# Attention: the turned sums and the row of maxima go to ScalarE and GpSimd, two sets of partial maxima, another order of TensorE's steps

## The chip, the cores and the metric

One core of one Trainium2 chip runs the whole program. The metric is the time of the device in microseconds (us) for one execution, a median over runs.

## The reference

A decoder layer on x of shape (1, 2048, 256): causal self-attention with 16 heads of 16, a cross-attention without softmax over 1601 context rows, and a mixture of 8 experts (two chosen per token) beside a shared one; a layer norm stands behind each. The change is in the self-attention alone:

```python
q = (x @ wq + bq).reshape(B, S, H, Dh).transpose(0, 2, 1, 3)
k = (x @ wk + bk).reshape(B, S, H, Dh).transpose(0, 2, 1, 3)
v = (x @ wv + bv).reshape(B, S, H, Dh).transpose(0, 2, 1, 3)
scores = jnp.einsum('bhqd,bhkd->bhqk', q, k) / jnp.sqrt(jnp.float32(Dh))
scores = jnp.where(causal[None, None], scores, jnp.float32(-jnp.inf))
attn = jax.nn.softmax(scores, axis=-1)
out = jnp.einsum('bhqk,bhkd->bhqd', attn, v)
```

S is 2048, H is 16, Dh is 16.

## The kernel before, in words

`project` forms q, k and v and the first maxima, `attend` does the attention of the 16 heads, `finish` the rest. Each is a block of its own; the next begins when every engine has ended the one before.

**The heads.** In `attend` a head's causal scores are cut into ten quads: a block of 512 queries (`qb`) by four tiles of 128 keys (`k0`). Quads 0, 2, 5 and 9 lie on the diagonal. A quad's scores are formed with keys on the partitions, in two halves, A and B. ScalarE turns each half into `probs` (an exponential, L735); on diagonal quads GpSimd zeroes the later keys (L689, `hide_later`). Three quads later (`LAG`) TensorE weighs the values with them (a W step, `weigh`, L792) and sums in `acc`; ScalarE copies `acc` when a block of queries is done (L740). The row of maxima, which keeps the exponential small, is a 49th row of the stacked q (`qstack`), so the scores of head h + 1 need it there first.

**The maxima.** For them the scores are formed once more, with queries on the partitions, in 35 pieces of up to 512 columns. Each piece takes a bank of a ring of three (`ring`, `NRING`); VectorE reduces it into `partial` (L178), and when the last piece of a head is in, reduces `partial` into `neg_max` (L871). Since there is one `partial`, it waits for its own `neg_max` before it takes a piece of the next head. TensorE transposes `neg_max` (M, L827), VectorE scales it into `max_row` (L876), and SP sends it by two DMAs into `qstack` (L667). Pieces of quads 6 to 9 belong to the head after next, the others to the next.

**The sums.** A head's four `acc_sb` blocks are folded by TensorE into a bank of the ring (F, L800, which ScalarE copies into `folded`, L747), transposed into another (T, L807), and normalised by VectorE: a reciprocal of the sums (L857) and a product into `attn` (L859).

**The order.** `STEPS` has one string a quad and is TensorE's order: A and B are the two halves of the scores, W a weighing of the quad three back, M, F, T as above, and small letters are pieces: w a whole one of 512 columns, n one of 384, d a whole one at the diagonal, p two of 256, q four of 128. M, F, T and the pieces go through the ring in that order: each waits until the bank three entries back has been read (`wait_taken`). VectorE takes its entries in the same order. TensorE works in two row groups (partitions 0 to 63 and 64 to 127) for scores and pieces, so that two of them can run beside each other; `given` picks the group for a piece.

**GpSimd and SP.** Beside `hide_later` GpSimd scales and splits the weights of the experts in three steps a head (`split_weights`, L695, L701, L704), dealt by `WEIGHTS_BEHIND` behind the diagonal quads of `qb` 0 (one step) and 2 (two steps). SP's queue is in order: the maxima's DMAs, the stack of four heads ahead, the split weights out and the next in.

The diff also touches `project`, which forms the first 50 pieces and head 0's maxima.

Of the kernel before, what the change touches and what calls it, by code (L numbers as in the profile page):

```python
# [8 lines left out]
H = 16  # L9
# [4 lines left out]
P = 128  # L14
# [40 lines left out]
def cut_pieces():  # L55
# [11 lines left out]
    for quarters, found in share.items():  # L67
# [25 lines left out]
STEPS = ("ABwwW", "wAwdBwW", "wAwBnWw", "ABwwWw", "AdwBwW",  # L93
         "wnWAwBnF", "wqABwwWwd", "AwWwB", "ApMTBwnW", "AdpBwWw")
# [41 lines left out]
TAKEN = [sum(x[0] != "fold" for x in ENTRIES[0:e + 1]) for e in range(len(ENTRIES))]  # L136
FOLDS = [sum(x[0] == "fold" for x in ENTRIES[0:e + 1]) for e in range(len(ENTRIES))]
LAST_PIECE = {g: e for e, (kind, g, _) in enumerate(ENTRIES) if kind == "piece"}
FIRST_PIECE = {g: e for e, (kind, g, _) in reversed([*enumerate(ENTRIES)]) if kind == "piece"}
# [32 lines left out]
def reduce_piece(nc, X, ALU, bank, partial, n):  # L172

    found = partial[:].rearrange("p t b -> p (t b)")
# [31 lines left out]
def decoder_layer(nc, x, xT, ctx_n, ctxT, wq, wk, wv, wo, b_qk, bv, bo, lm, w_all, gT, out):  # L206
# [15 lines left out]
    with whole:  # L222
# [10 lines left out]
        with ExitStack() as two:  # L233
            attn = two.enter_context(nc.sbuf_tensor("attn", [P, NT, DH + D], f32))
            with ExitStack() as three:
# [6 lines left out]
                partial = three.enter_context(nc.sbuf_tensor("partial", [P, NT, NQ], f32))  # L242
# [5 lines left out]
                w_scale = three.enter_context(nc.sbuf_tensor("w_scale", [P, 1], f32))  # L248

# [5 lines left out]
                        zeros16, ones16, fold, w_scale, stack_in, max_in)  # L255
                attend(nc, f32, f16, bf16, ALU, ACT, X, q_split, k_split, w_all, w_split_d, res, bo_rows, ident32,
                       attn, values, qstack, kstack, ident16, hide_keys, partial, neg_max, max_row,
                       zeros16, ones16, fold, w_scale, stack_in, max_in)
# [5 lines left out]
def project(nc, f32, f16, ALU, ACT, x, xT, ctx_n, ctxT, wq, wk, wv, wo, b_qk, bv, bo, lm, gT,  # L264
            q_split, k_split, res, wo_split, xm, gate_split, bo_rows, ident32, eps_col,
            attn, values, qstack, kstack, ident16, hide_keys, partial, X, neg_max, max_row,
            zeros16, ones16, fold, w_scale, stack_in, max_in):
# [4 lines left out]
    with es:  # L272
# [129 lines left out]
        def _(pool):  # L402
# [30 lines left out]
            nc.gpsimd.memset(w_scale[:], WSCALE).then_inc(pool_done, 1)  # L433
            nc.gpsimd.memset(fold[:], 0.0).then_inc(fold_set, 1)
# [5 lines left out]
            pool.wait_ge(pool_done, 9)  # L440
# [10 lines left out]
        def _(dve):  # L451
# [7 lines left out]
            def take_pieces(count):  # L459
                nonlocal taken  # L460
                for _ in range(count):
# [4 lines left out]
                    if m == NPIECE:  # L466
                        dve.wait_ge(first_max_found, 1)
                    reduce_piece(nc, X, ALU, piece_ps[m % NRING], partial, FIRST_PIECES[m]).then_inc(piece_done, 1)
                    taken += 1
                    if taken == NPIECE:  # L470
                        dve.wait_ge(piece_done, NPIECE)
                        nc.vector.tensor_reduce(out=neg_max[:], in_=partial[:], axis=X, op=ALU.max, negate=True).then_inc(first_max_found, 1)
# [108 lines left out]
def attend(nc, f32, f16, bf16, ALU, ACT, X, q_split, k_split, w_all, w_split_d, res, bo_rows, ident32, attn, values,  # L581
           qstack, kstack, ident16, hide_keys, partial, neg_max, max_row, zeros16, ones16, fold, w_scale,
# [5 lines left out]
    with es:  # L588
# [9 lines left out]
        inv = sb("inv", [P, 2, TPQ, NQ, 1], f32)  # L598
# [7 lines left out]
        ring_ready, ring_done, fold_copied = sem("ring_ready"), sem("ring_done"), sem("fold_copied")  # L606
        max_found = sem("max_found")
# [7 lines left out]
        def wait_taken(engine, e):  # L615

            if ENTRIES[e][0] == "fold":
                engine.wait_ge(fold_copied, FOLDS[e])
            else:
                engine.wait_ge(ring_done, TAKEN[e])  # L620
# [33 lines left out]
        def _(sp):  # L654
# [25 lines left out]
        def _(pool):  # L680
# [25 lines left out]

            done = 0
            for h in range(H):
                for qb in range(NQ):
# [6 lines left out]
                    if (h, qb) == (0, 1):  # L716
                        for g in range(NQ):
# [3 lines left out]
                                                    ALU.add).then_inc(biased, 1)  # L721
            assert done == 3 * H
            pool.wait_ge(biased, NQ)

        @block.scalar
        def _(act):
            def exps(h, s):
                quad = h * NQUAD + s
                for half in range(2):
                    first, w = span(s, half)  # L730
# [29 lines left out]
            copy_folded(H - 1)  # L760

# [91 lines left out]
        def _(dve):  # L853
            def normalise(bank, h):
                turned = bank[:].rearrange("p (t b v) -> p t b v", t=TPQ, b=NQ)
                tiles = attn[:].rearrange("p (b t) d -> p t b d", t=TPQ)
                nc.vector.reciprocal(inv[:, h % 2], turned[:, :, :, DH:DH + 1]).then_inc(inv_ready, 1)  # L857
                dve.wait_ge(inv_ready, h + 1)
                nc.vector.tensor_tensor(tiles[:, :, :, (h + 1) * DH:(h + 2) * DH], turned[:, :, :, 0:DH],  # L859
                                        inv[:, h % 2].broadcast_to([P, TPQ, NQ, DH]), ALU.mult).then_inc(ring_done, 1)  # L860

            for e, (kind, g, n) in enumerate(ENTRIES):
                bank = ring[e % NRING]
                if kind == "fold":
                    continue
                dve.wait_ge(ring_ready, e + 1)
                if kind == "piece":
                    reduce_piece(nc, X, ALU, bank, partial, n).then_inc(ring_done, 1)
                    if e == LAST_PIECE[g]:
                        dve.wait_ge(ring_done, TAKEN[e])  # L870
                        nc.vector.tensor_reduce(out=neg_max[:], in_=partial[:], axis=X, op=ALU.max,  # L871
                                                negate=True).then_inc(max_found, 1)
                        dve.wait_ge(max_found, g)
                elif kind == "max":
                    dve.wait_ge(max_in, g * MAX_DMAS)
# [966 lines left out]
```

## Time and profile before

| | us |
|---|---|
| median of 3 runs | 827.25 (825.53 to 828.89) |
| profiled execution | 824.61 |
| its span, first to last instruction | 822.9 |
| PE busy | 770.2 (94%) |
| VectorE (DVE) busy | 556.1 (68%) |
| ScalarE (ACT) busy | 513.6 (62%) |
| GpSimd (POOL) busy | 352.6 (43%) |

The loop over the heads runs from 87.5 to 454 us, `finish` behind it. Busy shares are means over the three stages. PE's busy time counts overlapping matmuls as modelled spans. "idle before" and the arrow behind it name what ended an engine's idle time.

### The profile page before, as it was taken

The page shows a single profiled execution, that of the slowest core. Times are in us where ns is not written, and L with a number is a line of the kernel's source. Part 1 is how long each engine was busy: PE and PEld are TensorE (multiplying, and loading weights), DVE is VectorE, ACT ScalarE, POOL GpSimd, SP SyncE. Part 2 cuts the span into 40 slices and gives each one's busy share as a digit, 9 for nine tenths or more (in the row PEclk, how much of TensorE's full clock was granted, in tenths as well). Part 3 has the DMA queues.
Part 4 walks back from the last instruction along what each step waited for, and adds up shares of the span by engine and source line. Part 5 has one row for each costly group of instructions (what it writes and reads, how often), then busy time and mean ns, then how long its engine had stood idle before and what let it go on. Part 6 is the DMA issues. An engine that isn't in the chain of part 4 may idle for free. (4 is left out here: it accounts for less than half of the span.)

```text
span 822.9 us, 18692 instructions
## 1 busy us (share of the span) xinstructions
PE 770.2 (94%) x6922; PEld 485.8 (59%) x6923; DVE 556.1 (68%) x1072; ACT 513.6 (62%) x756; POOL 352.6 (43%) x350
## 2 busy tenths in 40 slices
PE   5899899999999999999998897899999999999994
PEld 1367333444443344444332786788888888877883
DVE  3675799999999999999940796963333333322395
ACT  4441688888888888888898585434444444443443
POOL 5050587775566555666562121142333333301121
PEclk9999899999999999999999998999999999999997
DMA  8685334333444444434211897532222222221452
GB/s 303 111 186 206 116 114 145 137 113 132 147 143 154 155 156 154 146 112 169 102 74 58 354 310 219 225 96 66 79 76 76 76 76 76 59 59 53 113 190 77
DMA packets 68295, 111.38 MB, mean 135 GB/s; under 512 B 39453, under 2 KB 49854, under 8 KB 63870
## 3 DMA queue, kind: packets, MB, share of 16 engines
q1 hardware_dynamic: 63134, 93.36, 35.4%
q0 software_dynamic: 4752, 16.62, 5.9%
q10 hardware_dynamic: 336, 0.40, 0.4%
q8 instruction: 50, 0.82, 0.4%
q14 instruction: 23, 0.19, 0.1%
HBM read 66.60 MB, written 32.37 MB: 120 GB/s over the span
## 5 line engine op out<-in xcount | busy, mean ns | idle before, releaser
L178 DVE TENSOR_REDUCE partial<-ring 128x1 f32<-128x512 f32 (+3 forms) x510 | 309.6, 669 | 9.7 <-PE ring L160 7.0
L735 ACT ACTIVATE probs<-scores 128x1024 f32<-128x1024 f32 (+1 forms) x320 | 269.7, 901 | 54.1 <-PE scores L772 54.0
L1305 ACT ACTIVATE hid<-turned 128x512 f32<-128x512 f32 (+1 forms) x112 | 65.6, 586 | 160.6 <-PE turned L1466 131.5
L792 PE MATMUL acc<-probs,values 128*32 128x512 f32 (+2 forms) x1472 | 155.1, 492 | 1.5 <-ACT acc_sb L740 0.9
L160 PE MATMUL ring<-kstack,qstack 48*128 48x512 f16 x580 | 154.0, 354 | 1.7 <-DVE partial L178 0.6
L1491 PE MATMUL ops<-weights,work 128*128 (+1 forms) x1320 | 148.9, 273 | 2.6 <-issue 1.9
L1466 PE MATMUL turned<-mats,weights 128*128 128x256 f16 (+1 forms) x1344 | 144.2, 262 | 2.5 <-DMA mats<-attn 1.7
L1706 DVE TENSOR_TENSOR work<-hid,work 128x512 f16<-128x512 f32 (+1 forms) x112 | 76.8, 690 | 94.9 <-ACT work L1310 94.9
L1491 PEld LDWEIGHTS ops<-weights,work 128*128 128x128 f16 x1320 | 128.4, 98 | 18.8 <-issue 3.7
L772 PE MATMUL scores<-qstack,kstack 49*128 49x512 f16 (+3 forms) x640 | 131.4, 352 | 5.2 <-ACT probs L735 3.9
L1466 PEld LDWEIGHTS turned<-mats,weights 128*128 (+1 forms) x1344 | 122.4, 98 | 21.2 <-issue 3.9
L160 PEld LDWEIGHTS ring<-kstack,qstack 48*128 48x128 f16 x580 | 49.1, 93 | 130.2 <-DVE partial L178 109.8
L689 POOL TENSOR_SCALAR_AFFINE_SELECT probs<-probs 128x256 f32<-128x256 f32 x128 | 51.6, 409 | 160.5 <-ACT probs L735 160.5
L1230 POOL DMA_INDIRECT by_token<-attn,dest_u x39 | 38.8, 994 | 143.7 <-DVE attn L1715 137.9
L704 POOL TENSOR_TENSOR a_w_out<-a_w_in,a_w_out 128x2304 f16<-128x2304 f32 x16 | 73.1, 4570 | 0.1
L1310 ACT ACTIVATE work<-hid 128x512 f16<-128x512 f32 (+1 forms) x112 | 69.7, 622 | 4.7
L792 PEld LDWEIGHTS acc<-probs,values 128*32 128x32 f32 x1472 | 44.3, 108 | 36.7 <-issue 28.4
L695 POOL TENSOR_TENSOR a_w_in<-a_w_in,w_scale 128x2304 f32<-128x2304 f32 x16 | 64.4, 4028 | 1.3 <-DMA a_w_in<-w_all 1.1
L1715 DVE COPY attn<-ops 128x512 f32<-128x512 f32 (+1 forms) x20 | 13.6, 678 | 68.7 <-PE ops L1491 68.7
L772 PEld LDWEIGHTS scores<-qstack,kstack 49*128 49x128 f16 x640 | 38.2, 94 | 27.8 <-ACT probs L735 18.2
L1222 POOL DMA_INDIRECT attn<-rows_d,token_u x39 | 38.1, 978 | 30.2 <-issue 10.7
L167 PEld LDWEIGHTS ring<-hide_keys,ident 64*128 64x128 bf16 x458 | 39.9, 95 | 14.5 <-issue 0.6
(199 smaller groups left out, 712.7 us busy)
## 6 DMA issues: line engine op xcount, KB each, us to landing
a_w_in<-w_all SPq DMA_DIRECT2D x16, 1152.0 KB, 7.7
w_split_d<-a_w_out SPq DMA_DIRECT2D x16, 1152.0 KB, 5.4
weights<-w_split_d SPq DMA_DIRECT2D x6, 2048.0 KB, 19.7
weights<-w_split_d POOLq DMA_DIRECT2D x3, 2048.0 KB, 12.3
qstack<-q_split SPq DMA_DIRECT2D x72, 64.0 KB, 2.7
kstack<-k_split SPq DMA_DIRECT2D x72, 64.0 KB, 2.8
weights<-by_token SPq DMA_DIRECT2D x8, 512.0 KB, 6.9
attn<-xT SPq DMA_DIRECT2D x4, 512.0 KB, 8.1
```

The costliest lines, as they stand in the source:

```text
L160: mm = nc.tensor.matmul(bank[:, at:at + w], qstack[rows, slot, t * P:(t + 1) * P], kstack[rows, slot, c:c + w], start=True, stop=not diagonal)
L178: return nc.vector.tensor_reduce(out=found[:, places[0]:places[-1] + 1:step], in_=bank[:, 0:WIDTH[n]].rearrange("p (k w) -> p k w", k=len( ...
L695: nc.gpsimd.tensor_tensor(w_in[:, u % 2], w_in[:, u % 2], w_scale[:].broadcast_to([P, WU]), ALU.mult).then_inc(w_scaled, 1)
L704: nc.gpsimd.tensor_tensor(w_out[:, u % 2, 1], w_in[:, u % 2], w_out[:, u % 2, 0], ALU.subtract).then_inc(w_lo, 1)
L735: nc.scalar.activation(probs[:, quad % NPROBS, at:at + w], scores[half][:, first:first + w], ACT.Exp, scale=QK_SCALE).then_inc(exp_done, 1)
L772: nc.tensor.matmul(scores[half][:, at:at + w], kstack[used, slot, kt * P:(kt + 1) * P], qstack[used, slot, (qb + 1) * QB - w:(qb + 1) * QB ...
L792: mm = nc.tensor.matmul(acc[VW * group:VW * (group + 1), first_query:first_query + w], values[:, h, k0 + j], probs[:, quad % NPROBS, at:at ...
L1305: nc.scalar.activation(h32, hps[b].rearrange("p (j n) -> p j n", n=TW)[:, :, 0:w], ACT.Silu, scale=1.0 / WSCALE).then_inc(silu_done, 1)
L1310: nc.scalar.activation(hid[:, parity, 0, b * HB:(b + 1) * HB, 0:w], h32, ACT.Copy).then_inc(hid_hi, 1)
L1466: mm = nc.tensor.matmul(place.rearrange("p (g n) -> p g n", n=P), weights[:, a, bass.ds(at + (k * HID + (b * HB + j) * P), P)], turned_row ...
L1491: mm = nc.tensor.matmul(bank[:, i], hid[:, parity, a, j, i * P:(i + 1) * P], weights[:, c, bass.ds(at + (WE // 2 + j * D), D)], start=(m = ...
L1706: nc.vector.tensor_tensor(hid[:, parity, 1, chunks, 0:w], hid32[:, b % 2].rearrange("p (j n) -> p j n", n=TW)[:, :, 0:w], hid[:, parity, 0 ...
```

## The change

ScalarE now reads both transposed banks: `copy_max` scales the maxima into `max_row`, and `copy_turned` copies the turned sums into `sums`; both stand ahead of the second exponential of the quad that has M and T. GpSimd normalises (`normalise`): a power of -1, a wait, a product, behind the hiding of a head's last quad. VectorE keeps the pieces and `neg_max`. `partial` has two sets, by the head's parity, and `neg_max` is found behind the first piece that follows a head's last one. The one counter `ring_done` becomes four: `pieces_reduced`, `max_copied`, `turn_copied` and `fold_copied`. `STEPS` is another order of the same steps.

```diff
-STEPS = ("ABwwW", "wAwdBwW", "wAwBnWw", "ABwwWw", "AdwBwW",
-         "wnWAwBnF", "wqABwwWwd", "AwWwB", "ApMTBwnW", "AdpBwWw")
+STEPS = ("wABwwW", "wABwwW", "wAddBWw", "AwBwWw", "qABwwWw",
+         "nAWBwpF", "wABpnwW", "wwABwWw", "AnMTwBwWn", "AdBdwW")
...
+BEHIND_LAST = {e: g for g, last in LAST_PIECE.items()
+               for e in [min((n for n, x in enumerate(ENTRIES) if n > last and x[0] == "piece"), default=last)]}
...
-                partial = three.enter_context(nc.sbuf_tensor("partial", [P, NT, NQ], f32))
+                partial = three.enter_context(nc.sbuf_tensor("partial", [P, 2, NT, NQ], f32))
...
-                    if m == NPIECE:
-                        dve.wait_ge(first_max_found, 1)
...
-                    sp.wait_ge(ring_done, TAKEN[ENTRY_AT["max", h + 1, 0]])
+                    sp.wait_ge(max_copied, h + 1)
...
+            def normalise(h):
+
+                pool.wait_ge(turn_copied, h + 1)
+                nc.gpsimd.tensor_tensor(inv[:, h % 2], sums[:, h % 2, :, DH], minus_one[:].broadcast_to([P, NT]),
+                                        ALU.pow).then_inc(inv_ready, 1)
+                pool.wait_ge(inv_ready, h + 1)
...
+                nc.gpsimd.tensor_tensor(tiles[:, :, :, (h + 1) * DH:(h + 2) * DH], by_quad[:, :, :, 0:DH],
+                                        over.broadcast_to([P, TPQ, NQ, DH]), ALU.mult).then_inc(normalised, 1)
...
+                    if qb == NQ - 1 and h > 0:
+                        normalise(h - 1)
             assert done == 3 * H
+            normalise(H - 1)
+            pool.wait_ge(normalised, H)
...
+            def copy_max(g):
+                e = ENTRY_AT["max", g, 0]
+                act.wait_ge(ring_ready, e + 1)
+                act.wait_ge(max_in, g * MAX_DMAS)
+                nc.scalar.activation(max_row[:], ring[e % NRING][0:NT, 0:P], ACT.Copy, scale=QK_SCALE).then_inc(max_copied, 1)
+
+            def copy_turned(g):
+                e = ENTRY_AT["turn", g, 0]
+                act.wait_ge(ring_ready, e + 1)
+                if g >= 2:
+                    act.wait_ge(normalised, g - 1)
+                nc.scalar.activation(sums[:, g % 2], ring[e % NRING][:].rearrange("p (n v) -> p n v", v=VW)[:, :, 0:DH + 1],
+                                     ACT.Copy).then_inc(turn_copied, 1)
...
+                    if half == 1:
+                        for x in STEPS_OF[h][s]:
+                            if x[0] == "max":
+                                copy_max(x[1])
+                            elif x[0] == "turn":
+                                copy_turned(x[1])
...
+            def find_max(g):
+
+                dve.wait_ge(pieces_reduced, TAKEN[LAST_PIECE[g]])
+                if g >= 2:
+                    dve.wait_ge(max_copied, g - 1)
...
+                reduce_piece(nc, X, ALU, ring[e % NRING], partial, g, n).then_inc(pieces_reduced, 1)
+                if e in BEHIND_LAST:
+                    find_max(BEHIND_LAST[e])
```

## Rows read from the trace of the kernel before

**Rows 1.** Busy time of each engine, 150 to 400 us: PE, PEld, DVE, ACT, POOL.

```profile
150.00:400.00 250.00, 248.71 (x2424) 103.39 (x2420) 244.10 (x430) 209.89 (x276) 156.47 (x123) 1.00 0.40 137
```

**Rows 2.** Timeline of DVE: start us, us, what.

```profile
244.06 0.27 DVE L876 TENSOR_SCALAR max_row<-ring 16x128 f16<-16x128 f32 x1
...
244.91 15.79 DVE L178 TENSOR_REDUCE partial<-ring 128x1 f32<-128x512 f32 x26
260.74 0.22 DVE L871 TENSOR_REDUCE neg_max<-partial 128x16 f32<-128x64 f32 x1
261.29 3.18 DVE L178 TENSOR_REDUCE partial<-ring 128x1 f32<-128x512 f32 x5 [0.33 <-PE ring L160]
...
266.79 0.27 DVE L876 TENSOR_SCALAR max_row<-ring 16x128 f16<-16x128 f32 x1
```

**Rows 3.** Timelines of PE and DVE around one full weighing.

```profile
239.12 0.57 PE L160 MATMUL ring<-kstack,qstack 48*128 48x512 f16 x2
239.62 1.06 PE L792 MATMUL acc<-probs,values 128*32 128x512 f32 x8
240.62 0.39 PE L160 MATMUL ring<-kstack,qstack 48*128 48x512 f16 x2
...
239.77 1.97 DVE L178 TENSOR_REDUCE partial<-ring 128x1 f32<-128x512 f32 x3
```

**Rows 4.** Timeline around M and T of one head.

```profile
242.85 1.30 DVE L178 TENSOR_REDUCE partial<-ring 128x1 f32<-128x512 f32 x2
...
243.59 0.66 PE L807 MATMUL ring<-ident,folded 128*128 128x128 f32 x4
...
244.18 0.39 PE L772 MATMUL scores<-qstack,kstack 49*128 49x512 f16 x2
...
244.40 0.38 PE L160 MATMUL ring<-kstack,qstack 48*128 48x512 f16 x2
```

**Rows 5.** Timeline of PE in quad 5: pieces, the piece behind the weighing, the fold.

```profile
258.03 0.39 PE L160 MATMUL ring<-kstack,qstack 48*128 48x512 f16 x2
...
259.13 0.38 PE L160 MATMUL ring<-kstack,qstack 48*128 48x512 f16 x1
...
259.80 1.06 PE L800 MATMUL ring<-acc_sb,fold 128*32 128x512 f32 x8
```

**Rows 6.** Timeline of PE: from a weighing's end to the start of the next.

```profile
253.58 0.39 PE L160 MATMUL ring<-kstack,qstack 48*128 48x512 f16 x1
...
254.55 0.34 PE L788 MATMUL acc<-ones,zeros 128*32 128x128 bf16 x3
```

**Rows 7.** Groups by form, 150 to 400 us: the full exponential on ACT.

```profile
L735 ACT ACTIVATE probs<-scores 128x1024 f32<-128x1024 f32 x133 | 129.2, 1027 | 17.7 <-PE scores L772 17.6
```

**Rows 8.** Timeline of the tail, head 14 into head 15: ACT, DVE and PEld.

```profile
426.40 0.62 ACT L740 ACTIVATE acc_sb<-acc 128x512 f32<-128x512 f32 x1
...
424.43 0.28 DVE L876 TENSOR_SCALAR max_row<-ring 16x128 f16<-16x128 f32 x1 [4.33 <-PE ring L827]
...
428.16 0.20 PEld L772 LDWEIGHTS scores<-qstack,kstack 49*128 49x128 f16 x4 [0.84 <-DMA qstack<-max_row]
```

**Rows 9.** Timeline of DVE at the end of the attention.

```profile
453.46 0.26 DVE L857 RECIPROCAL inv<-ring 128x16 f32<-128x16 f32 x1 [8.38 <-PE ring L807]
453.75 0.42 DVE L859 TENSOR_TENSOR attn<-ring,inv 128x256 f32<-128x256 f32 x1
```

**Rows 10.** Groups by form of POOL (L1248 is a power); one line's durations min/median/max.

```profile
L1248 POOL TENSOR_TENSOR f_rstd<-f_veps,minus_half 128x2 f32<-128x2 f32 x7 | 5.8, 823 | 29.7 <-DVE f_veps L1755 21.2 <-DVE f_nmean L1756 8.5
...
L1248 POOL TENSOR_TENSOR f_rstd<-f_veps,minus_half 128x1 f32<-128x1 f32 x2 | 1.3, 630 | 1.0 <-DVE f_veps L1755 1.0
...
L444 POOL TENSOR_TENSOR values<-values,bv_rows x16: 717/721/726, 40.6 to 53.8; 128x256 f32<-128x256 f32 x16
```

**Rows 11.** Timeline of POOL: the split behind quad 0, quad 2's hiding.

```profile
249.96 4.57 POOL L704 TENSOR_TENSOR a_w_out<-a_w_in,a_w_out 128x2304 f16<-128x2304 f32 x1
254.48 0.77 POOL L689 TENSOR_SCALAR_AFFINE_SELECT probs<-probs 128x256 f32<-128x256 f32 x2
```

More of the change, by code:

```diff
@@ L135 @@
 ENTRY_AT = {x: e for e, x in enumerate(ENTRIES)}
-TAKEN = [sum(x[0] != "fold" for x in ENTRIES[0:e + 1]) for e in range(len(ENTRIES))]
-FOLDS = [sum(x[0] == "fold" for x in ENTRIES[0:e + 1]) for e in range(len(ENTRIES))]
+COUNT = {kind: [sum(x[0] == kind for x in ENTRIES[0:e + 1]) for e in range(len(ENTRIES))]
+         for kind in ("piece", "max", "fold", "turn")}
+TAKEN = COUNT["piece"]
 LAST_PIECE = {g: e for e, (kind, g, _) in enumerate(ENTRIES) if kind == "piece"}
+BEHIND_LAST = {e: g for g, last in LAST_PIECE.items()
+               for e in [min((n for n, x in enumerate(ENTRIES) if n > last and x[0] == "piece"), default=last)]}
 FIRST_PIECE = {g: e for e, (kind, g, _) in reversed([*enumerate(ENTRIES)]) if kind == "piece"}
@@ L169, in form_piece, with reduce_piece @@
     return mm
-def reduce_piece(nc, X, ALU, bank, partial, n):
-    found = partial[:].rearrange("p t b -> p (t b)")
+def reduce_piece(nc, X, ALU, bank, partial, head, n):
+    found = partial[:, head % 2].rearrange("p t b -> p (t b)")
     places = [t * NQ + c // QB for t, c, _ in PIECES[n]]
@@ L615, in wait_taken @@
         def wait_taken(engine, e):
-            if ENTRIES[e][0] == "fold":
-                engine.wait_ge(fold_copied, FOLDS[e])
+            kind = ENTRIES[e][0]
+            if kind == "piece":
+                engine.wait_ge(pieces_reduced, TAKEN[e])
+            elif kind == "max":
+                engine.wait_ge(max_copied, COUNT["max"][e])
+            elif kind == "fold":
+                engine.wait_ge(fold_copied, COUNT["fold"][e])
             else:
-                engine.wait_ge(ring_done, TAKEN[e])
+                engine.wait_ge(turn_copied, COUNT["turn"][e])
         def halves_of(s):
@@ L853, in _ @@
         def _(dve):
[L854 to L860, printed above, removed]
+            def find_max(g):
+                dve.wait_ge(pieces_reduced, TAKEN[LAST_PIECE[g]])
+                if g >= 2:
+                    dve.wait_ge(max_copied, g - 1)
+                nc.vector.tensor_reduce(out=neg_max[:], in_=partial[:, g % 2], axis=X, op=ALU.max,
+                                        negate=True).then_inc(max_found, 1)
             for e, (kind, g, n) in enumerate(ENTRIES):
-                bank = ring[e % NRING]
-                if kind == "fold":
+                if kind != "piece":
                     continue
+                if e == FIRST_PIECE[g] and g >= 3:
+                    dve.wait_ge(max_found, g - 2)
                 dve.wait_ge(ring_ready, e + 1)
[L867 to L875, printed above, removed]
-                    nc.vector.tensor_scalar(max_row[:], bank[0:NT, 0:P], QK_SCALE, None, ALU.mult).then_inc(ring_done, 1)
-                else:
-                    normalise(bank, g)
+                reduce_piece(nc, X, ALU, ring[e % NRING], partial, g, n).then_inc(pieces_reduced, 1)
+                if e in BEHIND_LAST:
+                    find_max(BEHIND_LAST[e])
 def address_first(engine, address):
```

27 lines of the change are left out of this document (17 added, 10 removed).

## The prediction

> **What bounds the kernel now.** I read the page first, then one row of busy times over 150 to 400 us, the part of the attention in which every head looks alike. VectorE is busy 244.1 of 250 us there, ScalarE 209.9, GpSimd 156.5; TensorE's clock is granted in full [rows 1]. TensorE's 248.7 us says little, since its matmul spans overlap. Next, VectorE's timeline of one head [rows 2]: 35 reductions of score pieces, `neg_max`, and at 244.06 the copy of the row of maxima with the reciprocal and the product of the turned sums behind it. From one copy of the maxima to the next (244.06 to 266.79) a head takes 22.73 us. `neg_max` is found in the loop for heads 1 to 15, so 14 such intervals lie between the first and the last.
>
> So VectorE sets the pace. But it doesn't set it alone. Its reductions follow each other by 0.60 us when they are fed; three of them show a span of 1.97 us where 0.60 + 0.60 + 0.68 = 1.88 would do [rows 3]. The missing 0.09 us is not listed as idle time, because the recorded spans (0.68) are longer than the pitch. It comes from TensorE: the ring has three banks, and a piece that is formed just before a weighing (W) holds up the next one. The loop [rows 3, 4]: a reduction ends and frees its bank, TensorE starts on it 0.13 us later (the second reduction of the pair that begins at 242.85 starts at 242.85 + 1.30 - 0.69 = 243.46; the turn starts at 243.59); 0.32 us from that piece to the weighing (the second of the pair from 239.12 starts at 239.12 + 0.57 - 0.39 = 239.30; W at 239.62); 1.00 us weighing; 0.43 us from the next piece's start to its reduction (240.62 to 241.05). That is 1.88 us, against 1.80 us for three reductions. VectorE and TensorE are balanced within 5%, and the three banks tie them together. A head's 22.73 us are 31 pitches of 0.605 and four of 0.48 (the 384-wide pieces), 20.7 us, plus 0.85 us of copy, reciprocal and product, 0.66 us around `neg_max` and the fold, and about 0.55 us of such small losses behind seven full weighings.
>
> **Part 1: VectorE sheds the row of maxima and the division.** Removed: 0.85 us a head (244.06 to 244.91) [rows 2]. What keeps it from being a gain is the ring. M and T (the transposes) each hold a bank that no longer gives VectorE work. In the new quad 8, "AnMTwBwWn", T reuses the bank of the piece before n, so it starts 0.13 us after that reduction ended; it takes 0.59 us (243.59 to the scores at 244.18); the next piece is ready 0.43 us after it starts [rows 4]. That is 1.15 us, and in it VectorE has only n, 0.48 us. It idles 0.67 us. The order of before shows the same limit: the piece after T starts at 244.40, so it could be reduced from 244.83, and it is reduced at 244.91. Without the three instructions VectorE would have waited for it anyway. Gain 0.85 - 0.67 = 0.18 us.
>
> **Part 2: two sets of partial maxima, `neg_max` one piece later.** Before: `neg_max` at 260.74, the next reduction at 261.29 [rows 2], 0.55 us plus 0.1 us for the last reduction to drain. But `neg_max` filled a hole: TensorE was folding (259.80 to 260.80) and the next piece could be reduced only from 260.80 + 0.43 = 261.2 [rows 5]. Now the wait is gone and the hole stays, and `neg_max` (0.18 us) comes behind it. In the new quad 5 the fold starts 1.87 us after the weighing of quad 4 ends, so the next piece is reduced from 1.87 + 1.00 + 0.43 = 3.30 us, while VectorE is done at 2.96: hole 0.34. 0.34 + 0.18 = 0.52 against 0.66: gain 0.14 us.
>
> **Part 3: the order of the steps.** Between two weighings TensorE needs at least what [rows 6] shows for "w A B w w": 253.58 to 254.55, 0.97 us, and then 1.00 us for the weighing: 1.97 us with three pieces of 1.81 us. Before, most such stretches with full scores had four pieces or one pair of scores. The new one has three pieces and both pairs in quads 1 and 7 (in quad 7 1.99, for it begins with two pieces). Then quad 6: w comes in the same row group as n, behind a bank that waits for ScalarE's copy of the fold; 0.14 us late. Losses behind weighings, summed over the ten stretches of the new order: 0.11 + 0.16 + 0.06 + 0.07 + 0.15 + 0.18 + 0.07 = 0.80, against 0.55: 0.22 us worse, taken with rounding. And quad 5, "nAWBwpF": before, w and n started at 258.03 and the piece behind the diagonal weighing at 259.13 [rows 5], so that VectorE was fed at 1.53 us, just as it had done w and n (0.43 + 0.60 + 0.48 = 1.51). Now A stands ahead of that weighing, which starts 0.20 us later, and the piece is fed at 1.75: 0.24 us idle. Per head: -0.18 - 0.14 + 0.22 + 0.24 = +0.14 us. The same by stretches of TensorE's time from weighing's end to weighing's end: W0 1.91, W1 1.97, W2 and W3 3.69, W4 2.49, W5 and W6 5.49, W7 2.00, W8 and W9 5.32, together 22.87. The walk is good to some 0.1 us; I take +0.1, times 14 = **+1.4 us**. Its bounds are -1.2 (nothing of the ring holds) and +0.3 (each hole 0.05 longer than read).
>
> **Part 4: ScalarE.** It takes on a 16x128 copy and a 272-element copy. By the 1024-wide and the 512-wide rows (1.03 and 0.62 us, 0.8 ns an element) [rows 7, 8] these are 0.3 and 0.42 us; from the nearest rows they lie between 0.27 (the same copy on VectorE) and 0.62 us. ScalarE has 22.73 x (1 - 209.9 / 250) = 3.6 us free a head, so in the loop they cost nothing. If that cover were gone they'd cost 0.7. Behind them on ScalarE waits the second exponential of quad 8; it must be there for the scores of quad 9, over 1 us of TensorE's work away. The row of maxima comes about 0.9 us later, for the first exponential of quad 8 goes ahead of it. From the end of its copy to scores that had waited for the DMAs it is 3.45 us in the tail (424.71 to 428.16) [rows 8], and in the new loop the copy ends 3.6 us before TensorE wants them. Hidden, by 0.15 us; if it isn't, each 0.1 us costs up to 1.4 in all.
>
> **Part 5: the tail, where nothing of VectorE's hides anything.** From 420 us on no pieces are left and ScalarE is the bound. There the maxima of head 15 arrive later: the copy ended at 424.71; now it follows the first exponential of quad 8, the last but one before ScalarE's 426.40 (by 0.95 us each from 424.5 to 425.45), and ends at 425.8. The scores were already waiting for it (0.84 us), ScalarE behind them too, so **+1.0 us**. The turned sums of head 14: **+0.4**. At the very end the chain was: last transpose, reciprocal at 453.46, product to 454.17 [rows 9]. New: ScalarE's copy 0.42, a 0.07 handover, GpSimd's power, 0.08, GpSimd's product 0.72 (the same 128x256 shape in L444) [rows 10]. The power over 16 elements isn't in the trace; nearest are powers over one and two elements, 0.63 and 0.82 us. Low end 0.6 (elements free), by their difference of 0.19 an element 0.63 + 15 x 0.19 = 3.5, and at the upper end 4 (a difference 0.03 larger, which two rows leave open). I take 3.5, since the two rows do grow. Chain: 0.42 + 0.07 + 3.5 + 0.08 + 0.72 = 4.8 against 0.7: **+4.1 us** (+1.2 at the low end). The whole rest of the kernel starts behind the block's end, so all of it counts. Tail: +5.5.
>
> A rule of the Trainium skill speaks against this part too: GPSIMD Engine Reference, section "Engine selection", has elementwise work on VectorE, with GpSimd about twice as slow for two inputs. This trace agrees, 0.72 against 0.42 us for the product. By the rule alone, with both instructions doubled, the end would grow by 1.2 us instead of 4.1, and the sum would be 831.
>
> **Part 6: GpSimd in the loop.** Its order becomes: hide the head's last quad, divide, hide quad 0, 4.57 us of weight splitting, hide quad 2 (254.48) [rows 11]. The division puts 3.5 + 0.08 + 0.72 = 4.3 us in front. Counted from the end of W9 of the head before, hiding its last quad ends at 0.2 (by the walk its exponential ends 0.3 before W9, and a hiding takes 0.4), the division at 4.6, quad 0's hiding at 5.4, the split at 10.0, quad 2's hiding at 10.7; TensorE wants it at 1.91 + 1.97 + 3.69 + 2.49 + 0.53 = 10.6. It is at the edge: I count 0; each 0.1 us of power above 3.4 costs up to 1.4 us in 14 heads. SP's queue waits on `max_copied` 0.9 us longer, and behind it stand the stack loads of four heads ahead, which have 60 us.
>
> **Sum.** +1.4 + 5.5 = +6.9 us. The profiled execution took 824.61 us (span 822.9), the median is 827.25; on the median that is 834.
>
> **Rivals.**
> (a) Faster: VectorE alone is the bound. Then a head loses 0.85 + 0.33 = 1.2 us, 14 x 1.2 = 16.5, minus 5.5 for the tail: 816. For it speaks 98% busy; against it the feeding times of part 1. It decides if the reduction behind T starts less than 0.2 us after n ends. The Trainium skill's Perfetto Trace Analysis, section "Identifying the Most-Contended Engine", would have it this way: improve the engine with the highest occupancy first; the time it leads to is this 816. Chance 0.25 (half the gain, 822, counted here).
> (b) Same: the power takes its low end and the order is a little better than walked (-0.1 a head): 2.5 - 1.4 = +1, 828. Chance 0.25.
> (c) Slower by GpSimd: power 4 us, quad 2's weighing late by 0.6 us in 14 heads, 8.4 + 7.4: 843. Chance 0.2.
> (d) The forecast, 830 to 838: 0.3.
>
> **Numbers.** Within 0.5% (4.1 us) is what the measurement can't tell from no change: the three runs spread by 3.4 us. Slower: (c) and (d), 0.5; same 0.25; faster 0.25. The range leaves out the best of (a) and the worst of (c): 817 to 844; the forecast's own is 830 to 838.
>
> **What would show it.** Right: VectorE's groups in the loop without L876, L857, L859, yet its timeline shows a gap behind n in quad 8 of 0.5 to 0.7 us released by PE, and one of 0.3 at the fold; busy share 94%; heads of 22.7 to 22.9 us; the power as a POOL row of 3 to 4 us; 5 us more between the last transpose and the next phase. Wrong: heads of under 22.3 us (part 1 or 3 fails), a power of under 1 us (part 5), or `acc` weighings that wait for GpSimd's hiding (part 6).

## The result, and the profile after

The changed kernel takes 832.0 us (median of 20 runs, 826.84 to 835.47), the kernel before in the same comparison 826.18 us (20 runs, 823.3 to 829.49). The ratio is 1.006, with a 95% interval of 1.0046 to 1.0075: a small loss, but one that the interval keeps apart from no change. The medians differ by 5.8 us. The profiled execution has a span of 827.6 us against 822.9: +4.7 us, which is what the traces have to explain.

The middle of the attention first, 150 to 400 us of the changed kernel, in the columns of [rows 1]:

```profile
150.00:400.00 250.00, 246.08 (x2428) 100.93 (x2420) 235.98 (x398) 217.72 (x299) 194.07 (x146) 1.00 0.42 137
```

VectorE fell from 98% to 94%, ScalarE rose to 87%, GpSimd to 78%. VectorE's timeline of one head says what the shed work brought; it answers to [rows 2]:

```profile
152.57 14.68 DVE L182 TENSOR_REDUCE partial<-ring 128x1 f32<-128x512 f32 x24 [0.60 <-PE ring L164]
167.43 1.29 DVE L182 TENSOR_REDUCE partial<-ring 128x1 f32<-128x512 f32 x2 [0.18 <-PE ring L164]
169.05 0.69 DVE L182 TENSOR_REDUCE partial<-ring 128x1 f32<-128x512 f32 x1 [0.32 <-PE ring L164]
169.66 0.21 DVE L906 TENSOR_REDUCE neg_max<-partial 128x16 f32<-128x64 f32 x1
169.78 4.88 DVE L182 TENSOR_REDUCE partial<-ring 128x2 f32<-128x512 f32 x8
175.26 4.90 DVE L182 TENSOR_REDUCE partial<-ring 128x1 f32<-128x512 f32 x8 [0.61 <-PE ring L164]
```

A head takes 175.26 - 152.57 = 22.69 us, where it took 22.73. The copy of the maxima, the reciprocal and the product (0.85 us) are gone, and in their place stands 0.60 us of idle time behind the piece n of quad 8, ended by TensorE. Two more holes, 0.18 and 0.32 us, stand in quad 5 and at the fold. From the first `neg_max` of the loop to the last it is 1.5 us less: 101.9 to 418.4 here, 101.9 to 419.9 in the trace of before. But most of that isn't a faster head. Every interval but the first and the last is 22.68 or 22.69 us here (one is 22.76), against 22.73 or 22.74 (one is 22.76): 0.5 us in twelve of them. The last interval is 21.79 us against 22.74, because the last `neg_max` has no next piece to wait for and stands right behind its head's last piece, where it always stood before. M stands behind the first scores of quad 8 in both orders and is the fairer mark: from head 1's M to head 15's it is 316.5 us (105.94 to 422.43), before 317.15 (106.91 to 424.06). The loop gained 0.7 us.

```profile
L906 DVE TENSOR_REDUCE neg_max<-partial x15: 207/210/220, 101.9 to 418.4; 128x16 f32<-128x64 f32 x15
```

The loss is at the end. These are the last steps of the attention and the first of `finish` (all engines, timeline); they answer to [rows 9]:

```profile
451.93 0.63 PE L854 MATMUL ring<-ident,folded 128*128 128x128 f32 x4 [0.80 <-ACT folded L793]
452.60 0.40 ACT L764 ACTIVATE sums<-ring 128x272 f32<-128x272 f32 x1 [0.81 <-PE ring L854]
453.07 2.90 POOL L720 TENSOR_TENSOR inv<-sums,minus_one 128x16 f32<-128x16 f32 x1 [2.06 <-ACT sums L764]
456.05 0.62 POOL L726 TENSOR_TENSOR attn<-sums,inv 128x256 f32<-128x256 f32 x1
...
457.18 3.65 PE L1397 MATMUL turned<-ident,attn 128*128 128x128 f32 x16 [4.62 <-PEq L592]
```

From the last transpose's start to the first matmul of the next stage it is 457.18 - 451.93 = 5.25 us; the trace of before has 1.71 (452.79 to 454.50). That is +3.5 us. The last row shows something else: 16 transposes in 3.65 us, where the kernel before needs 1.94 for the same 16. The windows of TensorE's granted clock (the column ahead of the last two) say why:

```profile
450.00:454.00 4.00, 1.70 (x12) 0.61 (x12) 0.00 (x0) 0.99 (x2) 1.86 (x3) 1.00 0.00 0
454.00:455.00 1.00, 0.00 (x0) 0.00 (x0) 0.00 (x0) 0.00 (x0) 1.00 (x1) 0.91 0.03 8
455.00:460.00 5.00, 2.82 (x14) 2.85 (x15) 0.00 (x0) 0.84 (x1) 3.30 (x14) 0.50 0.37 105
460.00:465.00 5.00, 4.24 (x21) 2.81 (x20) 2.45 (x2) 1.20 (x2) 0.00 (x0) 0.50 1.01 424
465.00:470.00 5.00, 5.00 (x47) 4.65 (x46) 3.85 (x11) 2.60 (x3) 0.00 (x0) 0.99 1.01 424
```

After TensorE had nothing to do for 4.62 us, its clock stood at half (1.2 GHz) from about 455 to 465 us. Before, it is granted in full there (1.00 from 450 to 465). From the start of `finish` to the first matmul of the experts (L1505, before L1466) it now takes 36.88 us (457.18 to 494.06), before 34.44 (454.50 to 488.94): +2.4 us.

One more wait stands in the last head, and the trace of before doesn't have it. GpSimd (timeline), and TensorE's weighing of quad 2:

```profile
427.00 2.90 POOL L720 TENSOR_TENSOR inv<-sums,minus_one 128x16 f32<-128x16 f32 x1
...
431.28 4.57 POOL L714 TENSOR_TENSOR a_w_out<-a_w_in,a_w_out 128x2304 f16<-128x2304 f32 x1
435.81 0.77 POOL L699 TENSOR_SCALAR_AFFINE_SELECT probs<-probs 128x256 f32<-128x256 f32 x2
...
436.62 0.75 PE L839 MATMUL acc<-probs,values 128*32 128x320 f32 x12 [0.61 <-POOL probs L699]
```

GpSimd's division pushes the split back, the split pushes the hiding of quad 2 back, and TensorE waits 0.61 us for it. In the loop the hiding is done in time (at 301.70 for a weighing at 302.40, in one head); in head 15 no pieces are left and TensorE comes sooner.

The balance of the spans, to 0.1 us:

- Up to head 1's M: -1.0. The attention begins at 86.35 us, before at 87.50. The first `neg_max` of `project` lies anywhere between 67.9 and 70.5 us in the traces with the changed `project`, at 69.2 and 70.6 in the two with the old one, so as far as can be told this is scatter.
- Loop, M to M: -0.7.
- From head 15's M to `finish`: +4.3 (30.44 to 34.75 us). The end chain is +3.5 of it, and +0.8 lies between head 15's first scores and its last fold. Of these, 0.5 had built up when ScalarE began quad 6 (12.73 us behind the first scores, before 12.24): the wait for GpSimd, less a little that the new order gains. The other 0.3 came by the copy of the turned sums: from the start of quad 6 to ScalarE's next copy of `acc` it is 5.89 us, before 5.61.
- Half clock: +2.4. Everything else: -0.4. Sum, but for rounding, +4.7.

### The profile page after: what moved, and what is told of

Read it like the earlier page. It is cut to its first block and busy times, and to the rows that moved or that the text cites. A ratio compares the mean times of both kernels' runs of the same rounds, so it can differ in the third digit from the quotient of the medians.

```text
span 827.6 us, 18736 instructions
## 1 busy us (share of the span) xinstructions
PE 769.2 (93%) x6922; PEld 483.9 (58%) x6923; DVE 543.3 (66%) x1025; ACT 522.2 (63%) x787; POOL 407.1 (49%) x383
## 5 line engine op out<-in xcount | busy, mean ns | idle before, releaser
L164 PE MATMUL ring<-kstack,qstack 48*128 48x512 f16 (+1 forms) x584 | 155.2, 352 | 2.1 <-PEq L277 0.9
L1505 PE MATMUL turned<-mats,weights 128*128 128x256 f16 (+1 forms) x1344 | 142.9, 260 | 3.1 <-DMA mats<-attn 2.3
L1505 PEld LDWEIGHTS turned<-mats,weights 128*128 (+1 forms) x1344 | 121.8, 98 | 21.2 <-issue 4.4
L819 PE MATMUL scores<-qstack,kstack 49*128 49x512 f16 (+3 forms) x640 | 129.0, 351 | 4.0 <-ACT probs L781 3.7
L164 PEld LDWEIGHTS ring<-kstack,qstack 48*128 48x128 f16 x584 | 46.9, 93 | 119.9 <-DVE partial L182 109.8
L171 PE MATMUL ring<-hide_keys,ident 64*128 64x128 bf16 x466 | 51.4, 203 | 0.0
```

The source lines that it names most:

```text
L164: mm = nc.tensor.matmul(bank[:, at:at + w], qstack[rows, slot, t * P:(t + 1) * P], kstack[rows, slot, c:c + w], start=True, stop=not diagonal)
L171: mm = nc.tensor.matmul(bank[:, at - P + a:at - P + b], ident16[rows, copy], hide_keys[rows, copy, a:b], start=False, stop=part == 1)
L819: nc.tensor.matmul(scores[half][:, at:at + w], kstack[used, slot, kt * P:(kt + 1) * P], qstack[used, slot, (qb + 1) * QB - w:(qb + 1) * QB ...
L1505: mm = nc.tensor.matmul(place.rearrange("p (g n) -> p g n", n=P), weights[:, a, bass.ds(at + (k * HID + (b * HB + j) * P), P)], turned_row ...
```

## The experiments

Each starts from the changed kernel unless said otherwise. "Mid-loop head" is the distance from one `neg_max` to the next around 240 to 265 us.

**The end on VectorE.** VectorE divides the last head, from the bank of the ring; ScalarE's and GpSimd's part in it goes.

```diff
-            normalise(H - 1)
-            pool.wait_ge(normalised, H)
+            pool.wait_ge(normalised, H - 1)
...
-            copy_turned(H - 1)
...
+            dve.wait_ge(ring_ready, e + 1)
+            nc.vector.reciprocal(over, turned[:, :, :, DH:DH + 1]).then_inc(last_inv, 1)
+            dve.wait_ge(last_inv, 1)
+            nc.vector.tensor_tensor(tiles[:, :, :, H * DH:(H + 1) * DH], turned[:, :, :, 0:DH],
```

> The changed kernel, with the last head's turned sums divided on VectorE straight from the ring's bank, as before the change. Theory (the end of the attention pays twice: 3.5 us of longer chain, and the 4.6 us in which TensorE idles are followed by 10 us at half clock, which cost another 2.4 us behind it): 5 to 6 us less than the changed kernel, so 0 to 1 us under the kernel before, and no stretch at half clock between 450 and 470 us. Rival 1 (the half clock stands by itself and has nothing to do with the idle): 3.5 us less, half clock stays. Rival 2 (the added time is in the loop): no more than 1 us less.

Measured: 824.84 us (12 runs) against 825.07 of before in the same comparison, ratio 0.9992 (0.9974 to 1.001). Its timeline, and its window with the clock:

```profile
452.96 0.63 PE L853 MATMUL ring<-ident,folded 128*128 128x128 f32 x4 [0.80 <-ACT folded L793]
453.63 0.26 DVE L924 RECIPROCAL inv<-ring 128x16 f32<-128x16 f32 x1 [34.02 <-PE ring L853]
...
454.67 1.94 PE L1407 MATMUL turned<-ident,attn 128*128 128x128 f32 x16 [1.08 <-PEq L592]
```

```profile
454.00:466.00 12.00, 9.69 (x86) 8.71 (x87) 7.58 (x17) 4.94 (x6) 2.37 (x17) 1.00 0.87 344
```

1.71 us again for the end, and the full clock. With the last head's division back on VectorE, nothing of the measured loss is left; 3.5 us of it were the chain and 2.4 the clock. (The wait of 0.6 us for GpSimd in head 15 stands in this trace too.)

**TensorE kept busy.** Four folds of head 15's sums again, behind its last transposes. They change nothing but what TensorE does while GpSimd divides.

```diff
+            for _ in range(4):
+                fold_sums(ring[ENTRY_AT["fold", H - 1, 0] % NRING], H - 1)
```

> The changed kernel, with TensorE folding the last head's sums four more times (4 us of matmuls whose output nobody reads) while GpSimd divides. The chain is as long as in the changed kernel. Theory (idle TensorE lets its clock fall, and the next stage starts at half clock): the half-clock stretch at 455 us goes, the next stage takes 34.4 us instead of 36.9 up to its first expert matmul, 2 to 2.5 us less in all. Rival (the clock falls for another reason): same time, half clock as before.

Measured: 828.91 us (12 runs), ratio 1.0037 (1.0017 to 1.0057), in the same comparison as the run above. Timeline:

```profile
452.75 3.64 PE L847 MATMUL ring<-acc_sb,fold 128*32 128x512 f32 x32
...
453.33 2.90 POOL L720 TENSOR_TENSOR inv<-sums,minus_one 128x16 f32<-128x16 f32 x1 [2.06 <-ACT sums L764]
...
457.45 1.94 PE L1399 MATMUL turned<-ident,attn 128*128 128x128 f32 x16 [1.05 <-PEq L592]
```

`finish` starts no earlier than in the changed kernel (457.45), yet the transposes take 1.94 us, the clock reads 1.00 from 454 to 466, and the first expert matmul comes at 492.09 for 494.06. Work that computes nothing won 2 us by the traces: a part of the loss is the clock, and not the wait. (By the medians the gain is of the same size, but the intervals of the two ratios, 1.0046 to 1.0075 and 1.0017 to 1.0057, overlap.)

**The old order under the new engines.** `STEPS` as before, the rest as changed.

> The changed kernel with the old order of TensorE's steps. My walk has the new order 0.46 us a head worse at quad 5 and behind the weighings, and the hole behind the turn a little larger in the old one (M and T, then the scores, then the piece: 0.77 for 0.60 us): heads of 22.4 to 22.5 us for 22.69, 3 to 4 us less in all than the changed kernel. Rival (the new order is needed for the division's move to pay): heads of 22.8 us or more, 2 us or more above the changed kernel.

Measured: 840.75 us (6 runs), ratio 1.0175 (1.0148 to 1.0203); mid-loop head 23.45 us. The expectation was wrong, and by more than any term of the prediction. Timeline around M and T:

```profile
246.72 1.94 ACT L781 ACTIVATE probs<-scores 128x1024 f32<-128x1024 f32 x2 [0.80 <-PE scores L819]
...
247.01 0.28 PE L874 MATMUL ring<-ident,neg_max 128*16 128x128 f32 x1
...
248.55 0.25 ACT L757 ACTIVATE max_row<-ring 16x128 f16<-16x128 f32 x1
...
248.85 0.33 PE L164 MATMUL ring<-kstack,qstack 48*128 48x384 f16 x1 [0.41 <-ACT max_row L757]
```

M is in its bank at 247.3, but ScalarE copies it only at 248.55, behind two exponentials: "AwWwB" forms quad 7's half B last, so its exponential and quad 8's first stand together ahead of the copy. The piece n takes M's bank and waits for it. In the new order ("wwABwWw") quad 7's halves are formed early, and the copy comes while the ring has no need of it yet. So the new order is what makes the move of the maxima bearable; whether it is a gain of its own, a run further down tells.

**Two of these undone.** The old order again, the maxima's copy back on VectorE, the end on VectorE, the turned sums on ScalarE and GpSimd.

> The old order, the maxima copied on VectorE as before the change, the turned sums on ScalarE and GpSimd, the last head divided on VectorE. The old order with both on ScalarE took 23.45 us a head, and there the piece behind the turn waited 0.4 to 0.9 us for ScalarE's copy of the maxima, which stands behind two exponentials. Theory (that wait is all that is wrong with the old order): the wait goes and heads take 22.6 to 22.7 us, 0 to 2 us under the kernel before. Rival (the turned sums on ScalarE cost the old order its time too): heads of 23.0 us or more.

Measured: 832.49 us (4 runs) against 826.37, ratio 1.0085 (1.0056 to 1.0115); mid-loop head 23.16 us. The wait for the maxima is gone and 0.3 us with it; it is not all. Timeline of what is left:

```profile
246.37 0.41 ACT L764 ACTIVATE sums<-ring 128x272 f32<-128x272 f32 x1
246.65 1.04 ACT L779 ACTIVATE probs<-scores 128x1024 f32<-128x1024 f32 x1
...
247.55 0.63 ACT L784 ACTIVATE acc_sb<-acc 128x512 f32<-128x512 f32 x1
247.74 0.10 PEld L816 LDWEIGHTS scores<-qstack,kstack 49*128 49x128 f16 x2 [0.19 <-ACT probs L779]
```

And VectorE's:

```profile
249.75 12.74 DVE L182 TENSOR_REDUCE partial<-ring 128x1 f32<-128x512 f32 x21 [0.37 <-PE ring L164]
```

The copy of the turned sums pushes quad 8's second exponential back, and the scores of quad 9 wait 0.19 us for it. Two us later VectorE has a hole of 0.37 us, where the kernel before has none: that is nearly all of the 0.43 us a head. The fold takes no more than before: its hole of 0.58 us and the 0.12 of `neg_max` make 0.70, where it was 0.66. That the wait of 0.19 us makes the hole is likely by its place, but not shown by a run. With the same engines in the new order a head takes 22.68 us (the last run below), so the move of the turned sums needs the new order too.

**The new order alone.** The kernel before with the new `STEPS`, nothing else (one run).

> The kernel before with the new order of TensorE's steps alone; VectorE keeps the copy of the maxima and the division. Theory: the new order is by itself the worse one where it stands between VectorE's work (0.24 us at quad 5, 0.2 behind the weighings, which the after profile shows as 1.53 for 1.35 and 1.97 for 1.8 us), so heads of 23.1 to 23.2 us for 22.73. Rival (the new order is better whoever takes the maxima): heads of 22.7 us or less.

Measured: span 827.2 us, mid-loop head 22.93 us: +0.20, half of what was expected. Under the old engines the new order costs. In this trace GpSimd, which doesn't divide, keeps nobody waiting in head 15: ScalarE begins quad 6 12.05 us behind the first scores, 0.7 less than in the changed kernel. And it gives the worth of the rest of the change: in the same order the move of the work and the two sets of maxima bring 22.93 to 22.69 us.

**T twice.** TensorE makes the four transposes of T twice in heads 0 to 14 (one run), so what VectorE waits for behind n gets longer, and nothing else does.

```diff
-                for t in range(TPQ):
+                for t in [*range(TPQ)] * (2 if h < H - 1 else 1):
```

> The changed kernel with the four transposes of T made twice in heads 0 to 14 (same result, 0.55 us more on TensorE a head). Theory (behind n, VectorE idles 0.6 us for TensorE and the three banks, so TensorE's time there is on the path): the hole grows from 0.60 to about 1.15 us and a head from 22.69 to 23.1 or 23.2. Rival (VectorE is the bound and TensorE has slack to catch up): heads stay within 0.1 us of 22.69.

Measured: span 836.3 us, mid-loop head 23.12 us. VectorE's timeline:

```profile
248.74 14.68 DVE L182 TENSOR_REDUCE partial<-ring 128x1 f32<-128x512 f32 x24 [1.04 <-PE ring L164]
```

The hole grew from 0.60 to 1.04 us and the head by 0.43: in this place TensorE's time is on the path.

**Work put into the hole.** First two copies of 128x128 fp32 on VectorE behind n (one run).

> The changed kernel with two copies of 128x128 on VectorE right behind the reduction of n that stands before M and T (about 0.4 us of work a head that nobody needs). Theory (VectorE idles there for TensorE): heads stay at 22.69 us, within 0.05. Rival (VectorE's work is the bound): heads of 23.0 to 23.1 us.

Measured: span 832.1 us. Between the first and the last, heads took from 22.67 to 24.5 us, which neither theory has. The group of the added copies, and a timeline of one pair:

```profile
L921 DVE COPY spare<-ident x28: 212/217/2518, 109.2 to 408.1; 128x128 f32<-128x128 f32 x28
```

```profile
246.10 2.11 POOL L712 CAST a_w_out<-a_w_in 128x2304 f16<-128x2304 f32 x1
...
246.90 1.52 DVE L921 COPY spare<-ident 128x128 f32<-128x128 f32 x2
```

The pair ends at 248.42, 0.21 us after GpSimd's cast does (248.21): the first copy was held until GpSimd had finished. Heads in which both copies took 0.21 us stayed at 22.68. The Trainium skill (SBUF — State Buffer, section "Who interferes with whom") has this as a rule: a VectorE copy that runs in a two-port mode and a GpSimd instruction exclude each other for an instruction's length, while an instruction with one SBUF input outside those modes isn't touched. The trace agrees, and the next run is the clean test.

```diff
+                if ENTRIES[e + 1][0] == "max":
+                    for i in range(2):
+                        nc.vector.tensor_reduce(out=spare[:, i], in_=ident32[:].rearrange("p (a b) -> p a b", a=4),
+                                                axis=X, op=ALU.max)
```

> The changed kernel with two throwaway reductions of 128 elements on VectorE behind n, in place of e5_in_hole's copies, which took 0.21 us alone and up to 2.5 us while GpSimd worked. Theory (the hole is idle time of VectorE, and only the copies' wait for GpSimd filled more than it): both take 0.2 to 0.25 us in every head and heads stay at 22.69 us. Rival (any work there costs): 23.0 us or more.

Measured: span 829.2 us (one run). Group of the added reductions, and VectorE's timeline:

```profile
L921 DVE TENSOR_REDUCE spare<-ident x28: 273/276/276, 107.9 to 402.6; 128x4 f32<-128x128 f32 x28
```

```profile
243.60 0.47 DVE L921 TENSOR_REDUCE spare<-ident 128x4 f32<-128x128 f32 x2
244.29 6.09 DVE L182 TENSOR_REDUCE partial<-ring 128x1 f32<-128x512 f32 x10 [0.22 <-PE ring L164]
```

None was held, and half a microsecond of work in each head left the loop where it was: first to last `neg_max` 316.2 us, in the changed kernel 316.5. The idle time was free. (The span's other 1.6 us lie outside the loop: the first `neg_max` is 1.1 us later.)

**M in quad 7.** To give VectorE pieces between M and T: "wMwABwWw" and "AnTwBwWn", the maxima copied ahead of quad 7's first exponential; with the end on VectorE.

> The last head divided on VectorE (e1_end), and M moved out of quad 8 into quad 7 behind its first piece, so that T has two pieces of VectorE's work before it, not one; ScalarE copies the maxima before the first exponential of quad 7. Theory (the hole is 1.15 us of latency minus the work of the two ring entries ahead of T): the hole of 0.60 us falls to 0.1 to 0.2, quad 7 pays 0.3 for M on TensorE; heads of 22.5 to 22.6 us, 1 to 3 us less than e1_end. Rival (the hole isn't set by the entries ahead of T): hole as before, heads of 22.9 us or more.

Measured: 827.59 us (10 runs) against 826.37, ratio 1.0021 (1.0009 to 1.0033); mid-loop head 22.85 us. VectorE's timeline:

```profile
243.41 2.46 DVE L182 TENSOR_REDUCE partial<-ring 128x1 f32<-128x512 f32 x4 [0.60 <-PE ring L164]
246.07 13.42 DVE L182 TENSOR_REDUCE partial<-ring 128x1 f32<-128x384 f32 x22 [0.21 <-PE ring L171]
```

The heads came out 0.3 us longer than expected, and near the rival's time, though not for its reason. The hole behind n did shrink, to 0.21 us, and another of 0.60 us opened in quad 7. By the waits of 150 to 400 us ScalarE, with its copy first in that quad, waited for M 10 times, 6.1 us in all. In both places that were tried, the bank that M takes from the pieces cost VectorE a hole.

**`neg_max` at once, and the maxima's copy on VectorE.** Both with the end on VectorE; the second has both edits.

```diff
-BEHIND_LAST = {e: g for g, last in LAST_PIECE.items()
-               for e in [min((n for n, x in enumerate(ENTRIES) if n > last and x[0] == "piece"), default=last)]}
+BEHIND_LAST = {last: g for g, last in LAST_PIECE.items()}
```

> e1_end (the last head divided on VectorE) with `neg_max` found right behind a head's last piece again, into the hole of 0.32 us that the fold leaves; the two sets of partial maxima stay. Theory (the hole at the fold is fixed by TensorE, so work put into it is free, and `neg_max` behind the next piece costs its 0.12 us): heads of 22.57 us for 22.68, 1.5 us less than e1_end. Rival (it's hidden where it is): 22.68 us, no difference.

> e11_max_at_once, and the row of maxima copied on VectorE, in the hole of 0.60 us behind n, as before the change; ScalarE and GpSimd keep the turned sums of heads 0 to 14. Theory (0.22 us of VectorE's work fit into that hole, and ScalarE has the time to spare): heads as in e11_max_at_once, within 0.05 us. Rival 1 (ScalarE's copy of the maxima was on the path): 0.1 us or more less a head. Rival 2 (VectorE has no room): 0.2 us more.

Measured: 826.42 us (12 runs) and 825.57 us (11 runs) against 825.53, ratios 1.0016 (1.0001 to 1.0032) and 1.0002 (0.9991 to 1.0013); both mid-loop heads 22.68 us. VectorE's timeline of the first and of the second:

```profile
259.19 1.29 DVE L181 TENSOR_REDUCE partial<-ring 128x1 f32<-128x512 f32 x2 [0.18 <-PE ring L163]
260.52 0.22 DVE L904 TENSOR_REDUCE neg_max<-partial 128x16 f32<-128x64 f32 x1
260.81 3.77 DVE L181 TENSOR_REDUCE partial<-ring 128x1 f32<-128x512 f32 x6
```

```profile
242.61 0.27 DVE L909 TENSOR_SCALAR max_row<-ring 16x128 f16<-16x128 f32 x1
243.29 14.68 DVE L181 TENSOR_REDUCE partial<-ring 128x1 f32<-128x512 f32 x24 [0.42 <-PE ring L163]
```

In the first, `neg_max` fills the hole at the fold and the 0.12 us it had taken behind the next piece are saved; the head is as long as ever, as the rival had it. In the second, VectorE has the maxima's copy back, its hole shrinks from 0.60 to 0.42 us, and the head is as long as ever. So VectorE has slack in both places. No version measured here beats the kernel before by what can be told.

## Why the prediction was right, and where it was off

834.0 us was forecast, 832.0 came; against the kernel before that is +6.9 forecast and +5.8 measured by the medians. The kernel is slower, by the case that was given as likeliest: the loop about even, the tail paying. But the closeness of the sum is partly luck: 2.9 us that the sum didn't have are covered by terms that came out lower. Its terms, in us, against what the traces show:

| term | forecast | measured |
|---|---|---|
| up to head 1's M (scatter) | 0 | -1.0 |
| loop, 14 heads | +1.4 | -0.7 |
| maxima of head 15 | +1.0 | 0.0 |
| turned sums of head 14 | +0.4 | +0.3 |
| wait for GpSimd in head 15, less the order's gain | counted as 0 | +0.5 |
| end chain | +4.1 | +3.5 |
| half clock behind it | not in the sum | +2.4 |
| the rest | 0 | -0.4 |
| span (each term rounded) | +6.9 | +4.7 |

**Part 1 was right.** The hole behind n was put at 0.67 us and is 0.60. T twice (hole 1.04, head +0.43) and the reductions in the hole (head unchanged) show that it is set by TensorE and the three banks and that VectorE's time in it is worth nothing.

**Part 2 was right in size and is worth nothing.** The hole at the fold was put at 0.34 us and is 0.32, `neg_max` at 0.18 and costs 0.12. But counting it as a gain on its own was wrong: with `neg_max` at once the head doesn't change.

**Part 3 was right in kind, its sum a little high.** Quad 5's hole was put at 0.24 us and is 0.18. (Its own losses behind weighings, 0.80 against 0.55, make 0.25 us; it took 0.22.) What is left when the three measured holes are taken out of the head is 22.69 - 22.73 + (0.85 - 0.60) + (0.66 - 0.32 - 0.12) - 0.18 = +0.25 us, where the losses behind weighings were put at 0.22. Summed: -0.25 - 0.22 + 0.25 + 0.18 = -0.04 us a head for the forecast +0.14. Read by holes, each step was within 0.1 us, and the head well inside the bounds of -1.2 to +0.3 us, but 14 heads make +1.4 into -0.7. The runs divide it otherwise: the new order alone costs 0.20 us where part 3 has 0.46, and parts 1 and 2 in that order bring 0.24 where they have 0.32. By the runs, the term that was put too high was the order's. What it did not see is what the old order would have done with ScalarE reading the maxima (+0.76 us a head, the run with the old order): it judged the order by TensorE's and VectorE's work and not by what stands ahead of the copy on ScalarE.

**Part 4 was right in the new order only.** ScalarE's copies take 0.25 and 0.40 us (put at 0.3 and 0.42). In the new order's loop the first costs nothing, since heads stay at 22.68 us with VectorE in its place; for the second no run tells it apart, and in the tail it cost 0.3 us. In the old order the first of them costs a wait in each head.

**Part 5 was right in its place, off in three sizes.** The power over 16 elements takes 2.90 us:

```profile
L720 POOL TENSOR_TENSOR inv<-sums,minus_one x16: 2900/2901/2943, 133.3 to 453.1; 128x16 f32<-128x16 f32 x16
```

With 0.63 and 0.82 us for one and two elements [rows 10] that is less than the straight line's 3.5, much more than 0.6. The prediction also weighed a rule of the Trainium skill (GPSIMD Engine Reference, section "Engine selection"), about twice VectorE's time for two inputs. For the product the trace has less, 0.62 against 0.42 us, 1.5 times. The power, which the rule doesn't name, took 2.90 us against the reciprocal's 0.26, so that doubling both instructions would have missed the chain. The +1.0 us for head 15's maxima was mis-sized: from M to the scores that wait for its row it took 4.11 us before (424.05 to 428.16) and takes 4.10 now. ScalarE, SP's queue and PEld, timeline:

```profile
423.48 0.25 ACT L757 ACTIVATE max_row<-ring 16x128 f16<-16x128 f32 x1
...
423.76 1.15 SPq L677 DMA_DIRECT2D qstack<-max_row  x2
...
426.53 0.17 PEld L819 LDWEIGHTS scores<-qstack,kstack 49*128 49x128 f16 x4 [0.84 <-DMA qstack<-max_row]
```

The copy of the maxima was expected 1.1 us later and came less late. From M's start (422.43) to the end of the copy it is 1.30 us, before 0.66: the copy is 0.64 later, not 1.1. From there to the scores it is 2.80 us and was 3.45 [rows 8]: issuing the two DMAs took SP 1.15 us and had taken 1.79. Why SP was quicker stays open; it wasn't tried.

**The missing term** is the clock. TensorE's idle time of 4.6 us in the chain was costed as a wait, and nothing asked what TensorE does behind a wait of this length. The end on VectorE and the four extra folds both take the half clock away, the second without a shorter wait: from the start of `finish` to the first expert matmul it is 34.47 and 34.64 us in them, 36.88 in the changed kernel and 34.44 before. So this is shown.

**Part 6 was right in the loop, and missed the last head.** GpSimd was put at the edge and counted as 0. The waits of 150 to 400 us (us in total, times, longest) have its lateness once, with 0.2 us:

```profile
PEld acc L839 <- POOL probs L699: 0.2, 1, 0.2
```

In head 15 it is over the edge by 0.61 us (436.62, in the rows above). The part walked a head with its pieces; the tail's head has none, and GpSimd's work in front of quad 2 is as long there.

**The rivals.** (a), VectorE alone the bound, falls with the hole of 0.60 us, far over the 0.2 from which it would have decided. The rule that goes with it (the Trainium skill, Perfetto Trace Analysis, section "Identifying the Most-Contended Engine") led the wrong way here: VectorE at 98% gave up 0.85 us a head, and the head got 0.04 shorter with the new order, 0.24 against the new order alone. (b) needed a power of 0.6 us; its other half, the slightly better order, did come. (c) needed a power of 4 us; what it foresaw for 14 heads, quad 2's weighing late by 0.6 us, came in head 15 alone.

## What to carry to other kernels

An engine at 98% is not the bound if its work comes through a short ring that another engine fills: list when each of its pieces could be had at the earliest, and see whether the instructions one takes off it stand in front of a hole. A step moved to another engine must be costed at the last turn of the loop too, where nothing hides it and what waits behind it on its new engine is wanted sooner; there the old engine can keep it. To compare two loops, measure between marks that stand in the same place in both. And when a wait of several microseconds is put in front of TensorE, look at the granted clock behind it.

## What was not expected of the hardware

- TensorE idle for 4.62 us ahead of `finish` read at half clock from about 455 to 465 us, which cost 2.4 us; idle for 1.08 us in the same place (the end on VectorE) it kept the full clock. The Trainium skill (TensorE: Matmul & The Clock Gate, section "What's actually happening") has an idle array fall to the lower level; the trace agrees.
- A 128x128 fp32 copy on VectorE from SBUF to SBUF takes 0.21 us alone and up to 2.52 us beside GpSimd; a reduction of the same tile kept to 0.28 at most.
- A power on GpSimd takes 0.63, 0.82 and 2.90 us for 1, 2 and 16 elements a partition.
